# A decoder layer on one core: another order of VectorE's work in the down projection, and a shorter norm on GpSimd

## The reference

```python
x = _layernorm(x + attention(x))          # 16 heads, relative positions
x = _layernorm(x + cross_attention(x, ctx))
x = _layernorm(x + ffn(x))

def ffn(x):                                # every activation is rounded to 16 bits by its own maximum
    x = act_qdq(x)
    up = act_qdq(x @ lpbq_dequant(w_up).T)
    gate = act_qdq(x @ lpbq_dequant(w_gate).T)
    gate = act_qdq(gate * fixed_qdq_u16(sigmoid(gate)))
    o = act_qdq(gate * up)
    return o @ lpbq_dequant(w_down).T      # 768 -> 256

def _layernorm(x, eps=1e-05):
    return (x - mean) / sqrt(var + eps)
```

## Time and profile before

| | |
|---|---|
| median of 3 runs | 1430.61 us |
| lowest and highest | 1427.94 and 1431.42 us |
| the profiled execution, its own time | 1430.84 us |
| its span in the profile | 1429.0 us |
| mean granted clock of TensorE | 0.947 |
| busy over the span | PE 1258.5, DVE 1056.4, ACT 974.0, POOL 346.8 us |

### The profile page before, as it was taken

One profiled execution on the slowest core, in us unless ns is written; L12 is line 12 of the kernel. 1 busy time (PEld: TensorE's weight loads), 2 busy tenths in 40 slices (PEclk: granted clock), 3 DMA queues, 4 the chain that ended last, 5 costly groups with the idle time before them and its releaser, 6 DMA issues. The chain is left out here.

```text
span 1429.0 us, 25354 instructions
## 1 busy us (share of the span) xinstructions
PE 1258.5 (88%) x8412; PEld 671.9 (47%) x8412; DVE 1056.4 (74%) x2561; ACT 974.0 (68%) x1690; POOL 346.8 (24%) x573
## 2 busy tenths in 40 slices
PE   8787999999999999999999999999997799910596
PEld 4343344334334334334434433437885687710586
DVE  4376788888887888888888888862574457999676
ACT  4434777777777777777777777773665558959661
POOL 4544121211211211212112121004552002420022
PEclk9989999999999999999999999999998899965798
DMA  8999977878888788697797786625321313825033
GB/s 251 303 335 259 252 210 224 227 206 244 225 220 228 214 244 219 195 266 214 208 252 211 227 226 183 211 75 166 97 75 45 133 59 119 315 84 217 1 104 103
DMA packets 263759, 273.14 MB, mean 191 GB/s; under 512 B 66222, under 2 KB 246990, under 8 KB 259534
## 3 DMA queue, kind: packets, MB, share of 16 engines
q1 hardware_dynamic: 261998, 268.39, 64.5%
q10 hardware_dynamic: 1632, 3.15, 0.7%
HBM read 153.69 MB, written 117.00 MB: 189 GB/s over the span
## 5 line engine op out<-in xcount | busy, mean ns | idle before, releaser
L604 ACT ACTIVATE pr<-scoresT 128x512 f32<-128x512 f32 x1024 | 548.1, 601 | 212.1 <-PE scoresT L856 151.9
L851 PE MATMUL scoresT<-qT,kT 99*128 99x512 bf16 (+7 forms) x1408 | 356.6, 327 | 6.0 <-DVE attn_out L741 2.3
L701 DVE TENSOR_REDUCE mx<-scores_for_max 128x1 f32<-128x888 f32 (+6 forms) x448 | 301.6, 673 | 0.0
L696 DVE CUSTOM_DVE_ANT_0 junk<-scores_for_max,win 128x200 f32<-128x200 f32 (+2 forms) x512 | 179.9, 351 | 159.1 <-PE scores_for_max L823 149.5
L699 DVE TENSOR_REDUCE mx<-scores_for_max 128x1 f32<-128x64 f32 (+6 forms) x448 | 277.4, 619 | 0.0
L869 PE MATMUL attn_out<-pr,vS 128*17 128x512 f32 x2048 | 271.2, 602 | 6.5 <-DMA vS<-v_all 6.3
L851 PEld LDWEIGHTS scoresT<-qT,kT 99*128 99x128 bf16 (+1 forms) x1408 | 107.4, 97 | 335.1 <-ACT rows L581 97.8
L856 PE MATMUL scoresT<-idf,win 128*128 128x128 f32 (+1 forms) x1024 | 200.7, 257 | 0.0
L478 POOL COPY rows<-rows 128x736 f32<-128x736 f32 x128 | 102.2, 798 | 381.2 <-ACT rows L581 381.2
L822 PE MATMUL scores_for_max<-kX,qT 64*128 64x512 bf16 x512 | 167.2, 384 | 4.0 <-DVE mx L701 3.0
L823 PE MATMUL scores_for_max<-kX,qX 64*128 64x512 bf16 x512 | 167.2, 384 | 0.0
(11 more groups left out here) (216 smaller groups left out, 1977.4 us busy)
## 6 DMA issues: line engine op xcount, KB each, us to landing
rel_table<-rows SPq DMA_DIRECT2D x128, 512.0 KB, 4.5
win<-rel_table SPq DMA_DIRECT2D x128, 512.0 KB, 5.4
up_raw<-xT_normed SPq DMA_DIRECT2D x6, 1536.0 KB, 10.0
xT_normed<-up_raw SPq DMA_DIRECT2D x6, 1536.0 KB, 6.6
qT<-q_parts SPq DMA_DIRECT2D x32, 256.0 KB, 7.5
kX<-k_parts SPq DMA_DIRECT2D x64, 128.0 KB, 4.9
kT<-k_parts SPq DMA_DIRECT2D x32, 256.0 KB, 5.6
q_parts<-shared SPq DMA_DIRECT2D x32, 192.0 KB, 4.5
```

What stands on the lines that cost most here:

```text
L604: nc.scalar.activation(pr[:, n % NPR, h, :], bank, ACT.Exp).then_inc(t_read, 1)
L696: last = nc.vector.tensor_tensor_reduce(junk[:, n % 2, 0:z - a], bank[:, a:z], win[:, T % NW, q4, h, u:u + z - a], 1.0, NEG, ALU.add, ALU. ...
L701: last = nc.vector.tensor_reduce(mx[:, T % 2, q4, h, 2:3], bank[:, z:L], AX.X, ALU.max)
L851: last = mm(bank[:, a:e], k[0:r], q[0:r, a:e], start=(n == 0), stop=not near and n == len(pieces) - 1, skip_group_check=True)
```

## The change

It does three things, all in the down stretch.

1. VectorE's order. The sums of block n now come as soon as the block's products are done, then the low parts of block n + 1, third 2, and of block n + 2, third 0, then the norm of block n, then the low part of block n + 2, third 1. Before, one low part lay between sums and norm.
2. In the last block the sums of the second half come before the norm of the first.
3. GpSimd makes only `rstd`, with two instructions instead of four (`norm_rstd_alone`). The cross attention keeps `norm_rstd`.

```diff
@@ -1023,6 +1023,14 @@
+        def norm_rstd_alone(pool, i, hf, wait):
+
+            wait(pool, l_aggr, i + 1)
+            k = 3 * 2 * NBLK + i - 2 * NBLK
+            nc.gpsimd.tensor_scalar(rstd[:, hf, :], mv[:, hf, :, 1], EPS, None, ALU.add).then_inc(l_eps, 1)
+            wait(pool, l_eps, k + 1)
+            nc.gpsimd.tensor_tensor(rstd[:, hf, :], rstd[:, hf, :], neg_half[:].to_broadcast([P, 4]), ALU.pow).then_inc(l_rstd, 1)
@@ -1068,7 +1076,7 @@
         feed_forward(nc, sem, spare, shared, h2d, ud, xd, wgh, wgl, wuh, wul, wdT, xr, ps, magic, coarse, step, inv, t_inv, amax,
-                     largest_of, scale_of, scale_pool, l_sum, norm_stats, norm_rstd, norm_apply, out)
+                     largest_of, scale_of, scale_pool, l_sum, norm_stats, norm_rstd_alone, norm_apply, out)
@@ -1920,19 +1928,22 @@
-            for n in range(NBLK):
-                low_part(n, 0)
-                if n >= 2:
-                    finish(n - 2, n - 2, (0, 1, 2, 3))
-                low_part(n, 1)
-                low_part(n, 2)
-                if n:
-                    begin(n - 1, n - 1, (0, 1, 2, 3))
+            for t in range(3):
+                low_part(0, t)
+            low_part(1, 0)
+            low_part(1, 1)
             last = NBLK - 1
-            finish(last - 1, last - 1, (0, 1, 2, 3))
+            for n in range(last):
+                begin(n, n, (0, 1, 2, 3))
+                low_part(n + 1, 2)
+                if n + 2 < NBLK:
+                    low_part(n + 2, 0)
+                finish(n, n, (0, 1, 2, 3))
+                if n + 2 < NBLK:
+                    low_part(n + 2, 1)
             begin(last, last, (0, 1))
+            begin(NBLK, last, (2, 3))
             finish(last, last, (0, 1))
-            begin(NBLK, last, (2, 3))
             finish(NBLK, last, (2, 3))
```

## The result

| | before | changed |
|---|---|---|
| median | 1429.98 us (7 runs) | 1424.95 us (7 runs) |
| lowest to highest | 1427.94 to 1433.12 | 1423.43 to 1428.89 |
| profiled execution, its span | 1430.84, 1429.0 | 1423.45, 1421.7 |
| first low part to the end of the span | 90.8 | 84.6 |

The ratio is 0.9955, with an interval from 0.9944 to 0.9966: about 6.4 us less by the ratio, 5.0 by the two medians. The predicted time was 1424.8, which is 6.1 less than the profiled execution of before.

A forecast was written before the change was run, and what follows sets the result against it. VectorE with GpSimd's chain in it was the bound. Gain 6.3 at block 6's sums, less 3.9 in the last block, plus 3.1 and 0.59, made 6.1 off 1430.84: 1424.8 us, range 1421.4 to 1427.4.

The forecast's parts named there:

- GpSimd, 0.59 a chain: Norm chain on GpSimd: dropping both shift instructions saves 0.59 us wherever the chain is waited for.
- The period, 8.79: VectorE's sums to sums in the down stretch: 8.79 us instead of 9.64, still above TensorE's 8.53.
- root free: Rival: low parts do not hold up GpSimd's root; TensorE's 8.53 bounds the period, 1421.1 to 1422.6 us; chance 0.12.
- both held: Rival: both low parts hold up both GpSimd instructions; period 9.06, 1426.4 us, or 1424.8 at full clock; chance 0.20.
- the cause that the prediction took from the gate stage: VectorE instructions with two SBUF operands, as low parts have, keep GpSimd out while they run.
- Where it starts: Block 1: sums at 1351.80, second sums at 1360.59 instead of 1362.63; TensorE stalls 0.8 once for third 2.
- TensorE's wait of 0.3 in each period: Each period VectorE leads and TensorE waits 0.26, seen as 0.3 ahead of third 2.
- The last block: TensorE pauses 2.8 before third 2, then a half-clock stretch costs 1.45; the block gives back 3.9 of the gain.
- the third rival: The prediction's own case without the half-clock stretch in the last block: 1423.3 us; chance 0.17.
- The end: Second half's sums to the end of the span: 7.16 less 0.59, 6.57; first half's norm costed at nothing.
- Hidden: Residual-row transfers take 14.5 of 17.6 us, 3.1 to spare, costed at nothing; ScalarE's parts lie beside TensorE as before.
- the sign of being wrong that the prediction named last: The prediction counts as wrong if the stretch before 1350 moves by more than 1 us.

The follow-up runs named there:

- e1: The kernel before with only GpSimd's two-instruction norm in place of the four-instruction one; 1426.53 us, ratio 0.9964.
- e3: The kernel before with only the second half's sums put ahead of the first half's norm in the last block; 1430.8 us, ratio 0.9994.
- e5: The changed kernel with third 0's low parts from block 2 on replaced by a maximum that reads one tile and writes one column; 1420.36 us.
- e4: The changed kernel with third 0's low parts from block 2 on made from one tile operand, less a scalar; 1421.86 us, ratio 0.9946.
- e2: The changed kernel with the four-instruction norm and the old order of the last two halves, so the new period order alone; 1430.38 us.
- e6: The changed kernel with block 7's third 2 low part moved ahead of the sums of block 6; 1422.69 us, ratio 0.9942.
- e7: The changed kernel with 22 unread matmuls in TensorE's pause ahead of the last block's third 2; 1423.78 us, ratio 0.9952.
- e10: The changed kernel run once more, with no edit; 1424.9 us, ratio 0.9954 to the kernel before.
- e8: The changed kernel with each norm one period later, a third residual buffer, and block 7's third 2 ahead of block 6's sums; 1420.24 us.

## Why the prediction was right

- **GpSimd, 0.59 a chain.** Right: in e1 the period falls from 9.64 to 9.06. Its price was hidden in the sum: alone it is worth 5.2, and the new order and the new tail alone, 2.1 each in the stretch, are too small to show in the run times. The text did not divide the gain by part, and one would have thought it the cover's.
- **The period, 8.79.** Measured 8.74. The root held up by the second low part until its end plus 0.90: measured 0.89. The wait of 0.94: 0.93 to 0.94. The second low part was to end 1.17 behind the first, because the add has its turn between them; it is 1.14 (1363.71 to 1364.85), as between two low parts with nothing of GpSimd's between them (1404.70 to 1405.84 in e3), so that turn cost VectorE nothing that shows, and the add still got in. The first two rivals (root free, both held) fall by the same rows. For the cause that the prediction took from the gate stage, two operands in SBUF, e5 shows that a cover without them lets the root through; e4 shows that it is not the whole rule.
- **Where it starts.** Sums at 13.6 from the first low part, second sums at 22.4: both as forecast (1359.46 less 1337.10). The stall of 0.8 in block 1 did not come in this profile, where TensorE ran at 0.50 for its first 5.4 us (1338.47 to 1343.9) and took up third 2 only at 1355.18; in e2, e6 and e7 it is 0.66 to 0.76. It costs the sum nothing, since VectorE leads.
- **TensorE's wait of 0.3 in each period.** The table of waits has none. The first matmul of third 2 comes 0.23 behind the one before it instead of 0.12, and the third takes 2.97 instead of 2.88 (1372.51 to 1375.48): 0.2 in all, as 8.74 less 8.53 asks, half of it ahead of the third and half within it.
- **Sums of block 6.** Forecast 66.35 (1404.54 less 1338.19), measured 66.07.
- **The last block.** Pause forecast 2.8, measured 2.51 (the view counts from the modelled end of the product before). A slow stretch followed, as in e10, and cost 1.47 (11.77 from the sums of block 6 to those of the second half, 10.30 in e7), forecast 1.45. But e2 shows that it need not have come, so this term was right with some luck; without it the third rival, 1423.3, would have been the time.
- **The end.** 6.57 from the last sums, measured 6.76: the add takes 0.29 beside the first half's norm instead of 0.23, and the end comes 0.1 later behind the last norm. That the half norm costs nothing because it has one tile operand was off by 0.06 only, but the reason given is the one that e4 refutes; in e3, with two chains close together, 0.5 was lost there.
- **Hidden.** The residual rows were never waited for, and ScalarE's waits cost nothing, as said.

The sum forecast a stretch of 84.7, and it was 84.6. The time of 1424.8 against the median of 1424.95 is luck in part: it is closer than the runs' own scatter of 4 to 5 us allows a sum to be, and the profiled execution, to which the sum was made, took 1423.45. Of its 7.4 us less, 6.2 are in the stretch; the first low part came 1.1 earlier (1337.10 against 1338.19). By its letter that is the sign of being wrong that the prediction named last, a move of more than 1 us ahead of 1350. The sign was set too tight: the start scatters by 5.9 between profiles, e3 starting 4.5 later than before with nothing changed ahead of it.

## What to carry to other kernels

Where one engine waits for a chain of small instructions on another, count the chain and not the busy share: each instruction of it is paid in full, every time. Before covering such a chain with other work, ask if the cover itself keeps the other engine out; a cover that does is worth only what it hides behind itself. Moving the consumer one period later, where memory allows another buffer, takes every chain but the last off the path, and with it the need to know most of these prices.

## What the runs showed of the hardware

- Where VectorE's low parts ran, GpSimd and VectorE took turns: the one that waited went in between two instructions of the other that stand back to back (1.11 for the add in the change, 1.05 for the shift in e2), and ended about 0.09 (a small one) or 0.89 (the root) behind the end of the instruction that held it up, its own time less 0.15. VectorE's two low parts ended no further apart for it (1.14 in the change and in e3).
- A subtraction with one tile operand in SBUF ran 128 x 1024 in 0.75 us against 1.22 with two, and kept GpSimd out all the same (e4); a maximum over as many in 1.21 did not (e5).
- With the norm straight behind the low part, the root took 1.98 instead of 1.86 (e8, in five periods), and beside the last block's norm the add took 0.29 instead of 0.23 (the change): the norm, with one tile operand, does not leave GpSimd quite alone either.
- With pauses of 1.8 to 2.5 us in the last block TensorE's clock fell to 0.50 for 3.4 us in five of six profiles, and not in the sixth (e2). It fell 0.9 to 1.5 us after TensorE had started again in four of them (1408.74 after 1407.46 in the change, 1411.35 after 1409.83 before), and in e3 0.3 ahead of the restart.
